# Expert scratch laid into the down weights' place, result stores issued by ScalarE, and routed transposes regrouped, in a Flamingo block with a mixture of experts

## Chip, cores and metric

The kernel runs on one core of a Trainium2 chip. The metric is the device time of one execution in microseconds (us). Engines are named as in the profile: PE is TensorE's matmul, PEld its weight load, DVE VectorE, ACT ScalarE, POOL GpSimd, SP SyncE, which only issues DMAs. A letter q behind an engine means its sequencer.

## The reference

All data is float32. `x` is 8 batches x 512 tokens x 256; `ctx` is 8 x 1024 x 256.

```
x = x + tanh(g0) * attention(layernorm(x), ctx)     # 16 heads of 64, layer norms, rope on the keys
    attn = softmax(clip(q @ k.T * 64**-0.5, -11, 11)); out = (attn @ v) @ Wo + bo
xf = layernorm(x)                                   # 4096 rows of 256
    scores = sigmoid(xf @ router_w.T)               # 64 experts in 8 groups
    the 4 best groups by the sum of their 2 best biased scores, then the 8 best experts in them
    tw = chosen scores / their sum * 2.5
routed = sum over chosen e of tw[e] * (relu(xf @ up_w[e])**2 @ down_w[e])    # 256 -> 128 -> 256
shared = relu(xf @ shared_up)**2 @ shared_down                               # 256 -> 512 -> 256
x = x + tanh(g1) * (routed + shared)
```

## The kernel before

One launch has four stages, each a block of its own in which every engine has its own program; all engines meet between two blocks.

**Setup** (to about 60 us) splits the attention's weights in two parts and turns the rope tables.

**Attention** (60 to 1906 us) goes through 8 batches `b`, in each through 8 pairs of heads `p`, and in each pair through 8 steps `c`. I write (p, c) for a step. A pair is projected while the pair before it attends. In a step PE makes the scores of one tile of 128 context rows (L903), ACT the exponential (L1047), POOL clamps it (L1139), DVE adds it to a sum (L1287), and PE multiplies the clamped tile of two steps earlier with the values (L968). Step 1 also makes the denominators (L976), steps 2 to 4 their reciprocal and the normalised output, steps 5 and 7 the output projection (L1004), which DVE adds to `x1` (L1210). All of it runs in program order on each engine, with semaphores between them.

The routing of the batch before, r = b - 1, is laid between these steps by hand: bias and statistics on DVE at (1, 6) to (2, 1), the reciprocal of the deviation on POOL at (2, 2) (L301, L304), the normalised rows `rows_now` on DVE at (2, 3) and (2, 6) (L312), their transposes on PE at (2, 4) and (3, 4) into the bank `ps_y` (L320), their copies on ACT, the router's product at (4, 4), ranks at (6, 4), and the choice and numbering of slots on DVE. The last of it, `finish_slots`, runs on DVE in pair 0 of the batch after (steps `FINISH`); it gives the row index of each token's 8 copies. Then POOL scatters the normalised rows of that batch into `rows_in_blocks` in DRAM, 32 indirect DMAs of 128 rows (L1119), at 32 steps of pairs 1 to 7, from b = 2 on. Before the first it waits, at the head of (1, 0), for the indices (`slotted`) and the rows (`rows_kept`). For the last batches `finish_slots` runs in the two closing half-pairs.

**Finish of the routing** (1906 to 2051 us): the last batch is routed on DVE (with PE and ACT for the products), POOL scatters the last two batches (64 indirect DMAs, L1387), and for all 8 groups of 512 rows g the shared expert runs: transposes (`turn`), the up product (L1426), relu and square on ACT (L1467, L1471), the down product (L1439), the sum on DVE (L1511). DVE also builds the table of which expert owns which block, and SP loads the up weights of all experts. PE's order is `turn(0)`, the router's transposes, `logits`, then `shared(0)`, `rank`, `shared(1)` to `shared(7)`. The scratch of this stage lies where the next stage puts `down_all`, all experts' down weights (64 x 128 x 256), so `down_all` can only be loaded once the stage is over. The weights of experts 0 to 3 alone are loaded before, into `router.rows`.

**Experts** (2051 to 2510 us): 320 blocks `i` of 128 rows. Blocks 0 to 63 are each expert's first, the rest belong to the expert named by the table. PE transposes the rows (L1770), multiplies by up two blocks later (L1739) and by down four blocks later (L1763). DVE takes relu (L1815) and square (L1819) and copies odd results out of PSUM (L1795), ACT copies the transposed rows (L1722), a table-chosen block's up weights (`now_up`, L1717) and even results (L1703). SP loads rows (L1661, 2 blocks each), loads `down_all` in 16 chunks of 4 experts at blocks 0, 2, ..., 30 (L1681), and stores results 4 blocks at a time (L1668), at block i those of i - 12. For blocks 0 to 47 DVE also puts gates in order (L1803 to L1808). POOL gathers each token's 8 results by 256 indirect DMAs (L1844) into a ring of 8, and DVE adds each to `x1` (L1788), starting at block 112: one per block, and the last 48 after the last block. A gather waits until the sum of 8 gathers before has freed its place.

Of the kernel before, what the change touches and what calls it, by code (L numbers as in the profile page):

```python
# [136 lines left out]
CHUNK = 4  # L137
LAG = 16
# [6 lines left out]
class Routed:  # L145

    def __init__(self, nc, ctx):
# [10 lines left out]
        self.first_loaded = ctx.enter_context(nc.semaphore("first_down_loaded"))  # L158
# [23 lines left out]
class Router:  # L182
# [36 lines left out]
    def scratch(self, nc, ctx, which, x_f, x_nat):  # L219
        def sb(name, shape, dt=F32):  # L220
            return ctx.enter_context(nc.sbuf_tensor(which + name, shape, dt))

        self.x_f, self.x_nat = x_f, x_nat
        self.stats = sb("r_stat", [P, GT, 6])
        self.moments = sb("r_moments", [P, GT, 2])
        self.rstd = sb("r_rstd", [P, 2, GT])
        self.prob = sb("r_prob", [P, GT, E_R])
# [20 lines left out]
        self.settle = sb("r_settle", [P, 1])  # L248
# [458 lines left out]
def attention(nc, pers, rope, ins, wqk_dram, wv_dram, xs_dram, slots_dram, gates_dram, router):  # L707


    with ExitStack() as ctx:  # L710
# [26 lines left out]
        router.scratch(nc, ctx, "a_", affine[:], rows_now[:])  # L737
# [139 lines left out]
        def _(pe):  # L877
# [11 lines left out]
            def step(g, m, c, project, attend, b=None, p=None):  # L889
# [98 lines left out]
                if routed(b) and c == 5 and p in (2, 3):  # L988
                    pe.wait_ge(router.copied, (b - 1) * 2 + p - 1)
# [20 lines left out]
        def _(act):  # L1010
# [16 lines left out]
            def step(g, m, c, project, attend, b=None, p=None):  # L1027
                jj = m % 2
                tail = exists(g - 2)
                if routed(b) and c == 5 and p in (2, 3):  # L1030
                    router.copy(act, b - 1, p - 2, y_flat)
# [52 lines left out]
        def _(pool):  # L1084
# [28 lines left out]
            places = [(p, c) for p in range(1, 7) for c in (0, 1, 4, 5, 7)] + [(7, 0), (7, 1)]  # L1113
            places.sort()
# [7 lines left out]
            def step(g, m, c, project, attend, b=None, p=None):  # L1122

                tail = exists(g - 2)
                if (p, c) == (1, 0) and not isinstance(b, int):
                    pool.wait_ge(router.slotted, b - 1)
                    pool.wait_ge(router.rows_kept, b - 1)
# [16 lines left out]
                if p is not None and not isinstance(b, int) and (p, c) in places:  # L1144
                    scatter(b, places.index((p, c)))
# [11 lines left out]
        def _(dve):  # L1157
# [55 lines left out]
            def route(b, p, c, g):  # L1213
# [16 lines left out]
                if (p, c) == (2, 3):  # L1230
                    router.normalise(dve, 0)
# [27 lines left out]
            def step(g, m, c, project, attend, b=None, p=None):  # L1259
# [53 lines left out]
def finish_routing(nc, pers, ins, kept, router, up, xs_dram, table_dram, slots_dram, gates_dram):  # L1313

    with ExitStack() as ctx:
        def sb(name, shape, dt=F32):
            return ctx.enter_context(nc.sbuf_tensor(name, shape, dt))
# [7 lines left out]
        x_last = sb("x_last", [P, GT, D])  # L1325
        x_f = sb("x_f", [P, 2, C2, TG])
        router.scratch(nc, ctx, "l_", x_f[:, 1], x_last[:])
        x_nat = sb("f_x_nat", [P, RING, GT, D])
        sup = sb("sup", [P, C2, E_S * P])
        sdn = sb("sdn", [P, E_S, D])  # L1330
        h_g = sb("h_g", [P, E_S, TG])
        h_r = sb("h_r", [P, 2, TG])
        total = sb("total", [P, T_T])
        cells = sb("cells", [P, 2, TOP_K, E_R])
        whole = sb("whole", [P, E_R], mybir.dt.int32)
        expert_no = sb("expert_no", [P, E_R])
        block_no = sb("block_no", [P, PACK])
        table_f = sb("table_f", [P, 2, PACK])
        table_t = sb("table_t", [P, 1], mybir.dt.int32)
# [12 lines left out]
        router.gathered()  # L1352

# [52 lines left out]
        def _(pe):  # L1406
# [10 lines left out]
            def shared(g):  # L1417
# [11 lines left out]
                if g + 1 < N_G:  # L1429
                    turn(g + 1)  # L1430
# [22 lines left out]
        def _(act):  # L1453
# [23 lines left out]
            for g in range(N_G):  # L1477
                shared(g)
                if g + 1 < N_G:
                    copies(g + 1)  # L1480
# [416 lines left out]
```

## Time and profile before

| | us |
|---|---|
| median of 3 runs | 2513.14 (2508.35 to 2518.33) |
| the profiled execution's own time | 2512.1 |
| its span in the profile | 2510.3 |
| PE busy | 2284.6 (91%) |
| DVE busy | 2041.2 (81%) |
| POOL busy | 1728.3 (69%) |
| ACT busy | 1522.5 (61%) |
| mean granted TensorE clock | 0.966 |

A busy share is a mean over the four stages; the windows in the section on rows give them apart. The 1.8 us between own time and span lie outside the span.

### The profile page before, as it was taken

What the parts mean: (1) busy time and instruction counts of PE and PEld (TensorE: products, weight loads), DVE (VectorE), ACT (ScalarE), POOL (GpSimd) and SP (SyncE); (2) the same over time, 40 slices, a digit from 0 to 9 for tenths busy, and PEclk for the clock granted to TensorE, in tenths of its full rate; (3) what the DMA queues carried; (4) which work ended last, traced back from release to release, by engine and by line L of the source; (5) the groups of instructions that cost most, each with busy time, mean ns of one, the idle gap of its engine ahead of it and who ended that gap; (6) DMA issues with size and microseconds to landing.
All of it is one profiled execution on the core that took longest, in us unless ns stands there. A gap on an engine that the chain in (4) does not pass through costs nothing. (4 is left out here: it accounts for less than half of the span.)

```text
span 2510.3 us, 40337 instructions
## 1 busy us (share of the span) xinstructions
PE 2284.6 (91%) x11366; PEld 1277.1 (51%) x11366; DVE 2041.2 (81%) x3571; ACT 1522.5 (61%) x2556; POOL 1728.3 (69%) x1515
## 2 busy tenths in 40 slices
PE   3999999999999999999999999999996989998990
PEld 2444445444444444454444444444544668987770
DVE  4778787988988898889889888988886759798884
ACT  4667666756666666667566756666662334766660
POOL 2777585588868876976788688868774600177776
PEclk9999999999999999999999999999997999999995
DMA  9533443111111112111112111111106438799994
GB/s 341 195 123 122 151 145 122 39 61 58 62 48 59 47 57 81 46 59 50 59 45 74 50 60 43 60 57 66 62 26 197 146 104 277 253 333 320 329 319 132
DMA packets 163582, 306.26 MB, mean 122 GB/s; under 512 B 19779, under 2 KB 99587, under 8 KB 160643
## 3 DMA queue, kind: packets, MB, share of 16 engines
q1 hardware_dynamic: 135234, 235.93, 27.5%
q0 software_dynamic: 24576, 67.14, 8.2%
q8 instruction: 105, 1.72, 0.3%
q14 instruction: 147, 1.20, 0.2%
q10 hardware_dynamic: 3520, 0.27, 0.1%
HBM read 173.51 MB, written 129.76 MB: 121 GB/s over the span
## 5 line engine op out<-in xcount | busy, mean ns | idle before, releaser
L1139 POOL TENSOR_SCALAR e<-e 128x1024 f32<-128x1024 f32 x512 | 706.9, 1381 | 320.7 <-ACT e L1047 267.5
L1047 ACT ACTIVATE e<-scores 128x1024 f32<-128x1024 f32 x512 | 524.7, 1025 | 424.3 <-PE scores L903 377.1
L1287 DVE TENSOR_TENSOR e_sum<-e_sum,e 128x1024 f32<-128x1024 f32 x384 | 589.7, 1536 | 100.7 <-POOL e L1139 100.4
L968 PE MATMUL ps_o<-e,v 128*64 128x512 f32 x2048 | 558.2, 624 | 7.8 <-POOL e L1139 7.7
L903 PE MATMUL scores<-q_t,k_t 64*128 64x512 f32 x3072 | 503.5, 433 | 15.1 <-DVE k_t L1277 11.8
L903 PEld LDWEIGHTS scores<-q_t,k_t 64*128 64x128 f32 x3072 | 253.4, 188 | 374.6 <-issue 282.7
L1844 POOL DMA_INDIRECT more<-results_in_blocks,index x256 | 246.0, 961 | 258.4 <-DMA results_in_blocks<-more 176.4
L1065 ACT ACTIVATE k_sw<-ps_k 32x512 f32<-32x512 f32 x512 | 301.3, 589 | 54.3 <-PE ps_k L944 49.2
L1119 POOL DMA_INDIRECT rows_in_blocks<-room,a_r_index_now x192 | 255.5, 1331 | 49.0 <-issue 49.0
L1131 POOL TENSOR_TENSOR k_c<-k_c,k_sw 128x512 f32<-128x512 f32 x128 | 192.6, 1505 | 46.7 <-DVE k_sw L1272 43.9
L944 PE MATMUL ps_k<-ctx_t,wqk 128*128 128x512 f32 x768 | 215.6, 417 | 0.9 <-DVE ctx_t L1163 0.3
L929 PE MATMUL ps_v<-wv,ctx_t 128*128 128x512 f32 x768 | 212.7, 412 | 2.4 <-ACT v L1058 2.4
L968 PEld LDWEIGHTS ps_o<-e,v 128*64 128x64 f32 x2048 | 102.1, 136 | 190.1 <-issue 156.3
L1763 PE MATMUL ps_out<-down_all,room 128*128 (+1 forms) x632 | 192.0, 386 | 0.7 <-DVE room L1819 0.3
L929 PEld LDWEIGHTS ps_v<-wv,ctx_t 128*128 128x128 f32 x768 | 135.0, 189 | 72.0 <-issue 45.5
L944 PEld LDWEIGHTS ps_k<-ctx_t,wqk 128*128 128x128 f32 x768 | 137.7, 193 | 65.8 <-issue 39.1
L1004 PE MATMUL ps_y<-wo,o_n 128*128 128x256 f32 x512 | 148.6, 414 | 13.2 <-DVE x L1210 9.6
L1739 PE MATMUL ps_hid<-x_nat,room 128*128 128x128 f32 x1024 | 157.3, 276 | 0.6 <-DVE room L1815 0.6
L1788 DVE SCALAR_TENSOR_TENSOR x<-more,gate,x 128x256 f32<-128x256 f32 x256 | 123.0, 480 | 42.5 <-DMA more<-results_in_blocks,index 41.5
L1722 ACT ACTIVATE x_nat<-ps_x 128x256 f32<-128x256 f32 x320 | 121.0, 379 | 59.4 <-PE ps_x L1770 56.0
L1277 DVE TENSOR_TENSOR k_t<-k_c,k_t 128x512 fp32r<-128x512 f32 x128 | 122.6, 958 | 41.2 <-ACT k_t L1073 41.0
L1004 PEld LDWEIGHTS ps_y<-wo,o_n 128*128 128x128 f32 x512 | 89.7, 195 | 130.4 <-issue 112.2
(288 smaller groups left out, 3510.5 us busy)
## 6 DMA issues: line engine op xcount, KB each, us to landing
rows_in_blocks<-room SPq DMA_DIRECT2D x16, 2560.0 KB, 10.5
x_nat<-rows_in_blocks SPq DMA_DIRECT2D x160, 256.0 KB, 5.3
results_in_blocks<-more SPq DMA_DIRECT2D x80, 512.0 KB
wqk<-wqk_pairs SPq DMA_DIRECT2D x65, 512.0 KB, 3.5
wv<-wv_quads SPq DMA_DIRECT2D x17, 1024.0 KB, 4.8
x_nat<-in_ctx SPq DMA_DIRECT2D x9, 1024.0 KB, 8.2
wo<-in_L_xattn_Wo SPq DMA_DIRECT2D x66, 128.0 KB, 3.4
down_all<-in_L_ffn_down_w SPq DMA_DIRECT2D x16, 512.0 KB, 7.7
```

What stands on the lines that cost most here:

```text
L903: mm = pe.matmul(scores[:, c % 2, hh * N:(hh + 1) * N], k_t[rows, att, kp, c * P:(c + 1) * P], q_t[rows, att, qp, :], start=(part == 0), s ...
L929: mm = pe.matmul(ps_v[:], ctx_t[:, a, cc, tile * P:(tile + 1) * P], wv[:, bb, cc], start=(k == 0), stop=(k == 5))
L944: mm = pe.matmul(ps_k[:], wqk[:, jj, bb, cc, 1], ctx_t[:, a, cc, half * N:(half + 1) * N], start=(k == 0), stop=(k == 5))
L968: mm = pe.matmul(ps_o[hh * DH:(hh + 1) * DH, :], v[:, tile, buf, hh * DH:(hh + 1) * DH], e[:, tile % 4, hh * N:(hh + 1) * N], start=(tile ...
L1004: mm = pe.matmul(ps_y[:, i, :], o_n[:, t * P:(t + 1) * P], wo[:, jj], start=True, stop=True)
L1047: act.activation(e[:, c % 4], scores[:, c % 2], ACT.Exp, scale=SCALE).then_inc(s_exp, 1)
L1065: st = act.activation(k_sw[to], ps_k[of], ACT.Copy)
L1119: pool.indirect_dma_start(xs_dram, bass.IndirectOffsetOnAxis(ap=router.index_now[:, t, k:k + 1], axis=0), router.rows[:, t], None).then_in ...
L1131: pool.tensor_tensor(k_c[:], k_c[:], k_sw[:], ALU.add).then_inc(s_turned, 1)
L1139: pool.tensor_scalar(e[:, c % 4], e[:, c % 4], EXP_HI, EXP_LO, ALU.min, ALU.max).then_inc(s_clip, 1)
L1287: dve.tensor_tensor(total, e[:, 0] if c == 2 else total, e[:, tile % 4], ALU.add).then_inc(s_sum, 1)
L1844: pool.indirect_dma_start(land[:, k], None, y_dram[0:blocks_of(b, k) * P, :], bass.IndirectOffsetOnAxis(ap=at, axis=0)).then_inc(y_in[k], 16)
```

## The change

1. **Scratch.** `down_all` is allocated ahead of the finish of the routing, and that stage's scratch is cut out of it, in the order in which it comes free. SP can so load chunk 0 after the scatters, chunks 1 to 3 after `last_kept` (ahead of the first rows), chunks 4 to 6 after the last group's transposes (`x_turned`), and chunks 7 to 15 in the experts' stage at blocks 0, 2, ..., 16. The extra load of experts 0 to 3 is gone.
2. **Stores.** ACT issues the stores of results, at block i those of i - 8.
3. **Relu** of blocks 0 to 63 goes from DVE to ACT, behind the copy of block i + 2.
4. **Routed rows** are normalised at (2, 4) and (2, 6) and both transposed in pair 3, at (3, 3) and (3, 4), with the wait for the first copy at (3, 4).
5. **Indices.** POOL waits for them at the first scatter, now (1, 1); the scatter of (1, 0) goes to (7, 5). The last part of `finish_slots` for the last batch but one goes from step 7 to step 2 of the closing half-pair.
6. **Order in the finish.** PE makes the up product of group 0 ahead of the router's transposes, and ACT its relu and square ahead of the router's copies.

```diff
-                if routed(b) and c == 4 and p in (2, 3, 4, 6):
+                if routed(b) and ((p, c) == (3, 3) or c == 4 and p in (3, 4, 6)):
                     pe.wait_ge(s_rec, g + 1)
-                    if p in (2, 3):
-                        router.turn(pe, b - 1, p - 2, y_flat)
+                    if p == 3:
+                        if c == 4:
+                            pe.wait_ge(router.copied, (b - 1) * 2 + 1)
+                        router.turn(pe, b - 1, c - 3, y_flat)
...
-            places = [(p, c) for p in range(1, 7) for c in (0, 1, 4, 5, 7)] + [(7, 0), (7, 1)]
+            places = [(p, c) for p in range(1, 7) for c in (0, 1, 4, 5, 7)][1:] + [(7, 0), (7, 1), (7, 5)]
...
-                if (p, c) == (1, 0) and not isinstance(b, int):
-                    pool.wait_ge(router.slotted, b - 1)
-                    pool.wait_ge(router.rows_kept, b - 1)
...
+                    if (p, c) == places[0]:
+                        pool.wait_ge(router.slotted, b - 1)
+                        pool.wait_ge(router.rows_kept, b - 1)
+                        pool.sem_inc(s_seen, 1)
                     scatter(b, places.index((p, c)))
...
-                if (p, c) == (2, 3):
+                if (p, c) == (2, 4):
                     router.normalise(dve, 0)
...
-                if attend and not project and c in FINISH:
+                if attend and not project and c in FINISH[:-1]:
                     finish_slots(B - 2, FINISH.index(c))
+                if not attend and not project and c == 2:
+                    finish_slots(B - 2, len(FINISH) - 1)
...
+        def load_down(sp, chunks):
+            for k in chunks:
+                sp.dma_start(down[:, k * CHUNK:(k + 1) * CHUNK],
+                             ins["down_w"][k * CHUNK:(k + 1) * CHUNK].rearrange("e p n -> p e n")).then_inc(kept.down_loaded[k], 16)
...
-            sp.dma_start(router.rows, ins["down_w"][0:CHUNK].rearrange("e p n -> p e n")).then_inc(kept.first_loaded, 16)
+            load_down(sp, range(0, ROWS_END))
+            sp.wait_ge(last_kept, 1)
+            load_down(sp, range(ROWS_END, ROUTING_END))
...
+            sp.wait_ge(x_turned, N_G * C2)
+            load_down(sp, range(ROUTING_END, RING_END))
...
             turn(0)
+            ups(0)
             router.turn(pe, last, 0, ps_r[:])
             router.turn(pe, last, 1, ps_l[:])
             router.logits(pe, last, ps_r[:])
-            for g in range(N_G):
-                if g == 1:
-                    router.rank(pe, last, ps_l[:])
-                shared(g)
+            downs(0)
+            router.rank(pe, last, ps_l[:])
+            for g in range(1, N_G):
+                ups(g)
+                downs(g)
...
-                e = i // XC * CHUNK
+                e = (i // XC + RING_END) * CHUNK
...
+            def store(i):
+                for parity in range(2):
+                    act.wait_ge(s_y[parity], (i + YC) // 2)
+                act.dma_start(four_blocks(y_dram, i),
+                              y[:, i % YR:i % YR + YC]).then_inc(y_stored[i % YR // YC], 16)
+
             for i in range(BLOCKS):
+                if i % YC == 0 and i >= 2 * YC:
+                    store(i - 2 * YC)
...
+                j = i - 2
+                if 0 <= j < E_R:
+                    act.wait_ge(s_up, j + 1)
+                    if j >= 2:
+                        act.wait_ge(s_g, j - 1)
+                    act.activation(act_r[:, j % 2], ps_h[:, j % 2, 0:P], ACT.Relu).then_inc(s_relu, 1)
...
-                dve.wait_ge(s_up, i + 1)
-                dve.tensor_scalar(act_r[:, i % 2], ps_h[:, i % 2, 0:P], 0.0, None, ALU.max).then_inc(s_relu, 1)
+                if i >= E_R:
+                    dve.wait_ge(s_up, i + 1)
+                    dve.wait_ge(s_g, i - 1)
+                    dve.tensor_scalar(act_r[:, i % 2], ps_h[:, i % 2, 0:P], 0.0, None, ALU.max).then_inc(s_relu, 1)
```

## Rows read from the trace of the kernel before

**Rows 1.** Windows by stage: length, busy (x instructions) per engine, clock, DMA share, GB/s
```profile
60.00:1906.00 1846.00, 1763.77 (x8249) 852.01 (x8248) 1561.16 (x2175) 1201.99 (x1685) 1397.79 (x1149) 0.98 0.22 73
1906.00:2051.00 145.00, 130.78 (x488) 88.52 (x488) 94.88 (x222) 51.16 (x87) 67.75 (x71) 0.93 0.45 147
2051.00:2124.00 73.00, 64.24 (x429) 55.57 (x430) 63.98 (x179) 28.33 (x82) 0.00 (x0) 0.95 0.85 293
...
2191.00:2452.00 261.00, 238.74 (x1650) 205.59 (x1648) 227.09 (x727) 168.62 (x513) 198.46 (x206) 0.99 0.95 321
```

**Rows 2.** Waits of PE in attention, 300 to 1860 us: total, times, longest
```profile
PE ps_y L320 <- DVE rows_now L312: 22.1, 7, 3.4
```

**Rows 3.** Timeline of PE in one batch, at (2, 4) and (4, 1)
```profile
1249.59 1.11 PE L320 MATMUL ps_y<-ident,rows_now 128*128 128x128 f32 x4 [3.12 <-DVE rows_now L312]
...
1290.62 1.08 PE L976 MATMUL ps_y<-e_sum,ones_dh 128*64 128x512 f32 x4 [1.21 <-DVE e_sum L1287]
```

**Rows 4.** Timeline of POOL in the same batch, clamps of (2, 3) and (2, 4)
```profile
1248.35 2.68 POOL L1139 TENSOR_SCALAR e<-e 128x1024 f32<-128x1024 f32 x2
```

**Rows 5.** Waits of POOL, 1242.9 to 1285.1 us, all there are
```profile
POOL rows_in_blocks L1119 <- issue: 1.7, 7, 0.3
POOL e L1139 <- ACT e L1047: 0.4, 2, 0.3
```

**Rows 6.** Timeline of POOL at (1, 0) of the same batch
```profile
1203.87 1.04 POOL L1139 TENSOR_SCALAR e<-e 128x1024 f32<-128x1024 f32 x1 [4.36 <-DVE index L543]
```

**Rows 7.** The page's group of the scatters in attention: busy, mean ns | idle before
```profile
L1119 POOL DMA_INDIRECT rows_in_blocks<-room,a_r_index_now x192 | 255.5, 1331 | 49.0 <-issue 49.0
```

**Rows 8.** Waits of POOL, 1160 to 1172 us, the end of a batch
```profile
POOL e L1139 <- ACT e L1047: 1.6, 1, 1.6
```

**Rows 9.** Timelines of DVE and PE at attention's end
```profile
1890.72 0.21 DVE L525 TENSOR_TENSOR room<-a_r_at_next,a_r_moved 128x64 f32<-128x64 f32 x1
...
1894.42 1.98 PE L976 MATMUL ps_y<-e_sum,ones_dh 128*64 128x512 f32 x4 [3.30 <-DVE e_sum L1287]
```

**Rows 10.** Timelines of PE and DVE at the start of the finish, and one load's landing
```profile
1922.03 9.70 PE L1426 MATMUL ps_h<-x_f,sup 128*128 128x512 f32 x16
...
1942.13 7.09 PE L1426 MATMUL ps_h<-x_f,sup 128*128 128x512 f32 x16
...
1922.69 0.29 DVE L351 TENSOR_SCALAR l_r_prob<-l_r_prob 128x256 f32<-128x256 f32 x1 [4.79 <-ACT l_r_prob L346]
...
1931.03 0.29 DVE L436 TENSOR_SCALAR l_r_taken<-l_r_gate 128x256 f32<-128x256 f32 x1
...
sdn<-in_L_ffn_shared_down_w SPq DMA_DIRECT2D x1, 512.0 KB, 4.8
```

**Rows 11.** Waits of PE, 2051 to 2191 us
```profile
PE ps_x L1770 <- DMA x_nat<-rows_in_blocks: 7.2, 4, 4.0
```

**Rows 12.** Windows of L1770 alone, two transposes a block
```profile
2062.10:2186.10 124.00, 40.71 (x208) 29.65 (x209) 0.98 0.81 273
2124.00:2186.10 62.10, 21.40 (x112) 15.94 (x113) 1.00 0.77 253
```

**Rows 13.** Timeline of DVE, the relu of two blocks that lie two blocks apart
```profile
2101.84 0.28 DVE L1815 TENSOR_SCALAR room<-ps_hid 128x128 f32<-128x128 f32 x1
...
2104.41 0.28 DVE L1815 TENSOR_SCALAR room<-ps_hid 128x128 f32<-128x128 f32 x1
```

**Rows 14.** Timeline of POOL, the first gather that waits for a sum
```profile
2191.05 0.94 POOL L1844 DMA_INDIRECT more<-results_in_blocks,index  x1 [7.64 <-DVE x L1788]
```

**Rows 15.** SP's issues of stores and of row loads: ns min/median/max
```profile
L1668 SPq DMA_DIRECT2D results_in_blocks<-more x80: 319/320/975, 2060.7 to 2451.7; - x80
...
L1661 SPq DMA_DIRECT2D x_nat<-rows_in_blocks x156: 319/730/2366, 2053.2 to 2438.5; - x156
```

**Rows 16.** Timelines of ACT and DVE around one block of the long loop
```profile
2300.20 0.42 ACT L1717 ACTIVATE room<-up_all 128x256 f32 x1 [0.52 <-issue]
...
2301.75 0.29 DVE L1815 TENSOR_SCALAR room<-ps_hid 128x128 f32<-128x128 f32 x1
```

More of the change, by code:

```diff
@@ L137 @@
 CHUNK = 4
+ROWS_END, ROUTING_END, RING_END = 1, 4, 7
 LAG = 16
@@ L217, in of_tile, with small @@
         return whole[t // LATER][:, t % LATER]
[L219 to L223, printed above, removed]
+    def small(self, sb):
         self.stats = sb("r_stat", [P, GT, 6])
@@ L736, in attention @@
         rows_now = sb("rows_now", [P, GT, D])
-        router.scratch(nc, ctx, "a_", affine[:], rows_now[:])
+        router.small(sb)
+        router.scratch(sb, affine[:], rows_now[:])
         minus_gate = sb("minus_gate", [P, 1])
@@ L987, in step @@
                         router.rank(pe, b - 1, y_flat)
-                if routed(b) and c == 5 and p in (2, 3):
-                    pe.wait_ge(router.copied, (b - 1) * 2 + p - 1)
+                if routed(b) and c == 5 and p == 3:
+                    pe.wait_ge(router.copied, (b - 1) * 2 + 2)
                 if routed(b) and c == 5 and p == 4:
@@ L1029, in step @@
                 tail = exists(g - 2)
-                if routed(b) and c == 5 and p in (2, 3):
-                    router.copy(act, b - 1, p - 2, y_flat)
+                if routed(b) and p == 3 and c in (4, 5):
+                    router.copy(act, b - 1, c - 4, y_flat)
                 if routed(b) and c == 5 and p == 4:
@@ L1473, in _ @@
             copies(0)
-            router.copy(act, last, 0, ps_r[:])
-            router.copy(act, last, 1, ps_l[:])
-            router.tanh(act, last, ps_r[:])
             for g in range(N_G):
                 shared(g)
+                if g == 0:
+                    router.copy(act, last, 0, ps_r[:])
+                    router.copy(act, last, 1, ps_l[:])
+                    router.tanh(act, last, ps_r[:])
                 if g + 1 < N_G:
@@ L1606, in _, with experts @@
             shared(7)
-def experts(nc, pers, ins, out, kept, router, up, xs_dram, y_dram):
+def experts(nc, pers, ins, out, kept, router, up, down, xs_dram, y_dram):
     with ExitStack() as ctx:
@@ L1632, in experts @@
         ps_y = ctx.enter_context(nc.psum_tensor("ps_out", [P, 4, N], F32))
-        down_loaded = [sem(f"down_loaded_{k}") for k in range(E_R // CHUNK)]
+        down_loaded = kept.down_loaded
         x_loaded = kept.x_loaded
@@ L1687, in _ @@
                     finish(b - 2)
-            for i in range(BLOCKS - 3 * YC, BLOCKS, YC):
-                store(i)
             finish(B - 2)
@@ L1877, in program @@
         up = ctx.enter_context(nc.sbuf_tensor("up_all", [P, E_R, D], F32))
-        finish_routing(nc, pers, ins, kept, router, up, xs_dram, table_dram, slots_dram, gates_dram)
-        experts(nc, pers, ins, out, kept, router, up, xs_dram, y_dram)
+        down = ctx.enter_context(nc.sbuf_tensor("down_all", [P, E_R, D], F32))
+        finish_routing(nc, pers, ins, kept, router, up, down, xs_dram, table_dram, slots_dram, gates_dram)
+        experts(nc, pers, ins, out, kept, router, up, down, xs_dram, y_dram)
 def kernel(**inputs):
```

86 lines of the change are left out of this document (48 added, 38 removed).

## The prediction

> **What bounds the kernel now.** I read the windows by stage first. Attention is 1846 us of 2510, with PE busy for 1763.8 of it, so it is PE's stage, with 82 us idle over 8 batches. The finish is 145 us with PE busy 130.8, its idle time at the start. In the experts' stage PE has 9 us idle in the first 73, and from 2191 us on it has 22 idle in 261, but there it isn't the bound: POOL issues 206 gathers in 261 us, one per 1.27 us [rows 1]. The timeline of POOL says since when: at 2191.05 us it last waited, for DVE's first sum [rows 14]. From there 248 of the 256 gathers follow each other; 248 x 1.27 from 2191 is 2506, the span's end but for the last landing and sum. So the end is the moment of the first sum, at block 112, plus 248 gathers. What the change saves ahead of block 112 comes through to the end; what it saves behind it is worth nothing, unless it delays the gathers.
>
> Then I asked for PE's waits in attention, and the largest is the one that part 4 is about: 22.1 us in 7 places for `rows_now` [rows 2]. The question is whether PE gets them back, and the timelines of PE and POOL of one batch answer it.
>
> **Part 4, transposes in pair 3.** PE is idle from 1246.47 us (1249.59 less 3.12) until `rows_now` is there, then makes the transposes (1.11) and the scores of step 5 [rows 3]. Without the wait it makes the scores at once, and then needs POOL's clamp of step 3. POOL starts that at 1248.35 and has it at about 1249.7 (half of 2.68) [rows 4]. So PE resumes 0.1 us later than now, but with the transposes (1.1) and scores (some 1.6 at the low clock after the gap) behind it: 2.7 us won, of which the transposes' 0.6 are paid again in pair 3. That is 2.1 us a batch, and 14.7 us in the seven batches that have routing. That is the upper bound, and I don't take it. From 1242.9 to 1285.1 us POOL never waits: 0.4 us for ACT, and 1.7 in the fixed gaps around its indirect DMAs [rows 5]. POOL is behind with 5 scatters a pair, the norms' reciprocals and the clamps, and at 1290.62 us PE waits 1.21 us for a sum of DVE that hangs on POOL's work of (3, 6) [rows 3]. An earlier PE doesn't make POOL earlier. Only the 0.4 us that POOL waited can be won, and some order between DVE and POOL: 0.5 us a batch. PE's lead turns into waits for clamps in pair 3. The exception is b = 1, where nothing is scattered yet and POOL has time: 2.1 us. Sum 6 x 0.5 + 2.1 = 5.1 us. The new wait for the first copy at (3, 4) is covered by the scores, key product and values product of that step, over 3 us against one copy; if ACT were late by more, PE would pay it.
>
> The Trainium skill (SBUF — State Buffer, "SBUF: two separate sides") says that DVE and GpSimd lock one pair of ports against each other, and the later one waits out the whole instruction. By that rule both saturated engines share one time here, so PE's lead would buy nothing at all, 2.1 us instead of 5.1. The trace leans that way: a clamp that takes 1.04 us elsewhere takes 1.34 in this stretch [rows 4, 6].
>
> **Part 5, the wait for indices.** POOL stands 4.36 us at (1, 0) for the index [rows 6], with the clamp of that step queued behind. PE's waits show nothing for it: its largest in attention is the one above. After the change the wait comes behind two clamps, when the index is there. Worth 0. The scatter moved to (7, 5) costs POOL 1.33 us and 0.26 of gap [rows 7], six times; POOL there still waits 1.6 us for ACT ahead of the clamp of step 5 [rows 8], and behind it PE stands at DVE's key split, so the scatter is covered. Without that cover it would be 6 x 1.6 = 9.6 us slower, the lower bound of this part. The last `advance` at the end stands between 1890.72 us and the sum before the product at 1894.42, on which PE waits 3.30 us [rows 9]: some 1.7 us of small DVE operations leave the path and fall into DVE's idle time behind the reciprocal. 1.7 us won, once.
>
> **Part 6, order in the finish.** Shared up weights land about 4.8 us after the stage's start [rows 10], at 1914 us. The up product of group 0, 9.70 us with the low clock of the start, then ends at 1923.7, where it now ends at 1931.7. The router's transposes, ACT's last square (ahead of the router's copies), the copies, the router's product and the tanh are five short steps in a row, which I put at 1 us each: DVE gets the tanh at about 1928.8 instead of 1922.69. The choice takes DVE 8.6 us, to the mask of L436, and brings it to 1937.4; PE spends that time on the down product, as large as an up product at full clock (7.1), and waits about 1 us. The ranks are 14 small products, which I put at 2.1 us, and the next up product starts at about 1939.6 instead of 1942.13 [rows 10]. 2.5 us won; between 0 (if DVE's scaling of gates, now behind a later mask, holds group 1) and 4. From there the stage is PE's and simply shifts.
>
> **Parts 1 to 3, experts.** From block 8 to 112 there are 208 transposes, 104 blocks, in 124 us. At the pace of the later half (56.5 blocks in 62.1 us, 1.10) they would take 114.3 [rows 12]: 9.7 us lost. Of PE's waits for rows, 7.2 us in four [rows 11], the longest, 4.0 us ahead of block 8, lies outside these 104 blocks. It stays: SP still issues four chunks ahead of the first row load. The low clock behind it (2.5 us) stays too. The other three (3.2 us) fall into the time of the chunks; seven of 16 chunks leave it, 3.7 MB, over 12 us at 293 GB/s [rows 1], so they go. The last 4 us are DVE's: with gate ordering its relus lie 2.57 us apart for two blocks, 1.29 a block against PE's 1.10 [rows 13]. The relu of 0.28 (0.31 with its gap) less gives 0.98, under PE. So 7.2 us can be won; ACT, busy 28.3 of 73 us [rows 1], has room for relu and stores. I take 7.0; the lower bound is 3 (only one of the two works).
>
> The stores: SP's issue takes 0.32 us [rows 15]. On ACT the wait for DVE's odd result and the issue stand ahead of `now_up` and the copy of block i. The loop closes once in four blocks: DVE's result, issue (0.32), `now_up` to relu 1.55 [rows 16], two blocks of DVE at 1.10 (227.1 us for 206 blocks), its result copy 0.4: about 4.3 us. POOL's pace leaves 4 x 1.27 = 5.1 [rows 1]. Covered by 0.8 us, so 0; the gathers set the time anyway.
>
> The Trainium skill (DMA: Bandwidth & Descriptors, "Issuing engines are not separate DMA queues") has it that another issuing engine saves only the issue time. By it the stores bring nothing; my sum has 0 for them too, and the third rival stands against both.
>
> **Sum.** 5.1 + 1.7 + 2.5 + 7.0 = 16.3 us. The profiled execution took 2512.1 us, 1.0 below the median of the runs; less 16.3 it is 2495.8. Its own range, from the bounds of the middle terms, is 2489 to 2503.
>
> **Rivals.**
> - *PE gets the whole gap back.* POOL's load isn't fixed, since clamps are shorter when DVE isn't at them: 14.7 instead of 5.1 us, 2486 us. For it: PE is busy 96% of the stage. Against it: [rows 5]. 0.15.
> - *The savings don't arrive.* The later mask delays the finish and SP's nine remaining chunks keep the early experts bound by transfers: 3 of 7.0, 0 of 2.5, 2 of 5.1: 2505 us. For it: the four chunks ahead of the first rows are unchanged. 0.18.
> - *ACT's stores hold the loop (slower).* An issue of SP's row loads takes 0.73 in the median and up to 2.37 us [rows 15]; if ACT's take longer than 0.32 + 0.8 = 1.1 us, the loop passes the gathers and sets the pace. At 2.0 us the four blocks take 6.0 instead of 5.1, 0.22 a block, over 206 blocks 46 us: 2542 us. Against it: the issues of the same stores on SP, median 0.32. 0.07.
>
> **How the numbers follow.** Forecast 0.60, rivals 0.15, 0.18, 0.07. Below 0.5%, 12.6 us, a measurement of this kernel can't tell a difference; the limit is 2500.5 us. Faster: 0.9 of the forecast and the first rival, 0.69. Same: the rest of the forecast and most of the second, 0.23. Slower 0.08. The range of 8 in 10 goes from the first rival's time to the second's: 2485 to 2507.
>
> **What would show it.** PE's wait for `rows_now` gone, with waits for clamps (L968 on L1139) grown in pair 3, and a batch's period down by 0.5 and not by 2 us; POOL's first wait at (1, 1) near 0; group 1's up product 2.5 us earlier behind the stage's start; blocks 8 to 112 in about 117 us, with the 4 us wait ahead of block 8 still there; gathers at 1.27 us. Wrong it would be by a gather pace over 1.3 us (ACT's stores), or by a batch's period down by 2 us (POOL not the bound).

## The result, and the profile after

The changed kernel takes 2522.2 us in the median of 9 runs (2517.5 to 2525.7), the kernel before 2512.7 beside it: a ratio of 1.0042, 95% interval 1.0031 to 1.0052. It is 9.5 us slower, where 16 us faster was forecast. The profiled execution's own time is 2521.93 us, its span 2520.2, which is 9.9 over the span before. The windows by stage, which answer to [rows 1]:

```profile
60.00:1911.00 1851.00, 1766.42 (x8250) 850.12 (x8248) 1559.41 (x2175) 1203.63 (x1686) 1386.48 (x1149) 0.98 0.21 73
...
2196.00:2457.00 261.00, 233.95 (x1621) 198.43 (x1620) 226.00 (x710) 155.37 (x504) 197.27 (x203) 1.00 0.95 316
```

The last row is the first finding: 203 gathers in 261 us, where there were 206, and PE is busy for 234.0 us of it, where it was 238.7. The long stretch at the end has become slower, though nothing was to change in it.

I cut both traces at five events: PE's denominators in the last whole pair, PE's first instruction of the finish and of the experts, the first gather that waits for a sum, and the last gather.

| us | before | after | difference | forecast |
|---|---|---|---|---|
| to the last whole pair's denominators | 1869.5 | 1876.1 | +6.6 | -5.1 |
| from there to the finish | 40.9 | 39.2 | -1.8 | -1.7 |
| finish | 140.8 | 138.6 | -2.1 | -2.5 |
| experts to the first waiting gather | 139.9 | 141.9 | +2.1 | -7.0 |
| the gathers (247 intervals) | 312.7 | 317.7 | +5.0 | 0 |

Two rows are as forecast, and three have the wrong sign or a cost where none was seen. I found two causes. The first row by itself doesn't show one: in eleven more profiles of kernels without part 4 the last whole pair's denominators come anywhere from 1869.1 to 1878.9 us. What singles part 4 out is the time with one line of it undone (a4) and the sum of pairs 2 and 3, both below.

**Attention.** PE's waits from 300 to 1860 us, where [rows 2] came from:

```profile
PE ps_o L969 <- POOL e L1138: 22.9, 18, 2.6
PE ps_y L977 <- DVE e_sum L1290: 20.1, 15, 2.6
```

The 22.1 us for `rows_now` are gone, but PE's waits for the clamp grew from 6.0 to 22.9 us, and those for the sum from 11.9 to 20.1. The timeline of PE in the batch of [rows 3] shows where:

```profile
1251.86 1.98 PE L969 MATMUL ps_o<-e,v 128*64 128x512 f32 x4 [2.08 <-POOL e L1138]
...
1268.10 1.38 PE L977 MATMUL ps_y<-e_sum,ones_dh 128*64 128x512 f32 x4 [2.29 <-DVE e_sum L1290]
```

And DVE in the same stretch, before and after:

```profile
1247.60 1.93 DVE L312 TENSOR_SCALAR rows_now<-x,a_r_moments,a_r_rstd 128x256 f32 x2 [0.91 <-POOL a_r_rstd L304]
```

```profile
1251.93 2.07 DVE L1290 TENSOR_TENSOR e_sum<-e_sum,e 128x1024 f32<-128x1024 f32 x1 [2.22 <-POOL e L1138]
1253.92 1.16 DVE L312 TENSOR_SCALAR rows_now<-x,r_moments,r_rstd 128x256 f32 x2
```

The normalisation used to fill DVE's wait for the clamp. Moved one step on, it leaves 2.22 us of DVE idle and stands in the busy stretch behind it. Then the windows of pair 2 (to its denominators) and pair 3 of one batch, first before, then after; the eighth column is the granted clock:

```profile
1003.37:1033.66 30.29, 26.13 (x116) 11.58 (x114) 25.04 (x39) 16.59 (x24) 26.57 (x27) 0.89 0.13 45
1033.66:1058.59 24.93, 23.74 (x116) 10.55 (x114) 22.14 (x26) 17.67 (x27) 22.92 (x19) 1.00 0.17 58
```

```profile
1003.54:1033.85 30.31, 23.46 (x112) 10.11 (x108) 25.21 (x39) 17.32 (x24) 26.78 (x27) 0.99 0.14 48
1033.85:1061.11 27.26, 27.18 (x118) 12.22 (x118) 21.42 (x26) 16.54 (x25) 20.92 (x19) 0.89 0.13 41
```

Pair 2 takes 30.3 us in both: DVE and POOL set it. Pair 3 takes 27.26 instead of 24.93, with PE busy 27.18 of it at a mean clock of 0.89. Over the six batches with scatters pair 2 went from 182.0 to 181.8 us in all and pair 3 from 149.6 to 156.1, together from 331.6 to 337.9. In the twelve profiles of kernels without part 4 this sum is 330.5 to 333.7, in the four with part 4 as changed (the changed kernel, a1, a3, f2) 335.5 to 338.6: these don't overlap.

**Experts.** Blocks 8 to 112, transposes alone, beside [rows 12]:

```profile
2064.60:2191.10 126.50, 40.90 (x208) 28.00 (x209) 0.99 0.73 243
```

It took 124.0 us before and was to take 117. What PE waits for from 2190 to 2460 us was nearly all DMA (18.9 us, 21 times); after:

```profile
PE ps_x L1809 <- ACT x_nat L1757: 26.7, 51, 0.6
```

Every fourth block PE waits half a microsecond for ACT's copy. The timelines of one such place, of DVE, ACT and PE, show the loop behind it:

```profile
2299.83 0.42 DVE L1834 COPY more<-ps_out 128x256 f32<-128x256 f32 x1
...
2300.33 0.33 ACTq L1735 DMA_DIRECT2D results_in_blocks<-more  x1
2301.21 0.42 ACT L1752 ACTIVATE room<-up_all 128x256 f32 x1 [2.02 <-PE ps_hid L1782]
2301.53 0.36 ACT L1757 ACTIVATE x_nat<-ps_x 128x256 f32<-128x256 f32 x1
...
2302.05 0.41 PE L1809 MATMUL ps_x<-ident,x_nat 128*128 128x128 f32 x2 [0.55 <-ACT x_nat L1757]
...
2302.94 0.29 DVE L1856 TENSOR_SCALAR room<-ps_hid 128x128 f32<-128x128 f32 x1 [0.50 <-PE ps_hid L1782]
...
2304.97 0.41 DVE L1834 COPY more<-ps_out 128x256 f32<-128x256 f32 x1
```

From one result copy of DVE to the next but one it is 5.14 us: 0.50 to the issue, 0.88 from there to `now_up` (the issue's 0.33 and 0.55 in which ACT also loads the table's register), 1.73 to relu, 2.03 to the next copy. Four gathers at 1.266 us are 5.06. So the loop, not POOL, sets the pace: 317.7 / 247 = 1.286 us a gather.

### The profile page after: what moved, and what is told of

The parts are those of the page before. It is cut to its first block and busy times, and to the rows that moved or that the text cites. A ratio compares the mean times of both kernels' runs of the same rounds, so it can differ in the third digit from the quotient of the medians.

```text
span 2520.2 us, 40661 instructions
## 1 busy us (share of the span) xinstructions
PE 2285.4 (91%) x11366; PEld 1266.0 (50%) x11366; DVE 2025.4 (80%) x3507; ACT 1521.7 (60%) x2620; POOL 1719.5 (68%) x1515
## 3 DMA queue, kind: packets, MB, share of 16 engines
q14 instruction: 150, 1.22, 0.2%
## 5 line engine op out<-in xcount | busy, mean ns | idle before, releaser
L1068 ACT ACTIVATE k_sw<-ps_k 32x512 f32<-32x512 f32 x512 | 301.3, 589 | 58.1 <-PE ps_k L945 53.1
L1121 POOL DMA_INDIRECT rows_in_blocks<-room,r_index_now x192 | 252.7, 1316 | 50.6 <-issue 47.9
L1130 POOL TENSOR_TENSOR k_c<-k_c,k_sw 128x512 f32<-128x512 f32 x128 | 186.0, 1453 | 41.9 <-DVE k_sw L1275 39.0
L1752 ACT ACTIVATE room<-up_all 128x256 f32 x256 | 106.8, 417 | 124.2 <-PE ps_hid L1782 108.7
L945 PEld LDWEIGHTS ps_k<-ctx_t,wqk 128*128 128x128 f32 x768 | 138.4, 193 | 66.3 <-issue 39.2
L1809 PE MATMUL ps_x<-ident,x_nat 128*128 128x128 f32 x640 | 124.8, 277 | 38.4 <-ACT x_nat L1757 33.3
```

What stands on the lines that cost most here:

```text
L945: mm = pe.matmul(ps_k[:], wqk[:, jj, bb, cc, 1], ctx_t[:, a, cc, half * N:(half + 1) * N], start=(k == 0), stop=(k == 5))
L1068: st = act.activation(k_sw[to], ps_k[of], ACT.Copy)
L1121: pool.indirect_dma_start(xs_dram, bass.IndirectOffsetOnAxis(ap=router.index_now[:, t, k:k + 1], axis=0), router.rows[:, t], None).then_in ...
```

## Experiments

Each was timed beside the kernel before on its chip; the ratio is to that. Where two kernels are compared by stages, these are cut from their profiles as above. On two of the chips the kernel before took 2658.7 and 2651.3 us; there I read ratios, the attention and the blocks ahead of 64 alone (the last section says why).

### One part alone, or undone

The kernel before with parts 4 and 5 alone (a1) and with part 2 alone (a2), by the lines of the diff above; the changed kernel with the stores taken from ACT's program and put back into SP's (a3):

```diff
-                if i % YC == 0 and i >= 2 * YC:
-                    store(i - 2 * YC)
...
+                if i % YC == 0 and i >= 3 * YC:
+                    store(i - 3 * YC)
```

And the changed kernel with one line back (a4):

```diff
-                if (p, c) == (2, 4):
+                if (p, c) == (2, 3):
                     router.normalise(dve, 0)
```

> The kernel before with parts 4 and 5 alone (the attention). Theory: the normalisation moved from (2, 3) to (2, 4) leaves DVE idle ahead of the sum of step 3 and comes back as a wait of PE for the sum at the denominators; it carries the whole loss of the attention, which ends 4.8 us later in the trace after (1915.2 instead of 1910.4), and nothing behind it moves: 2512.7 + 4.8 = 2517.5 us. Rival, the attention's delay in the trace comes from the new place of the scratch (parts 1 to 3 and 6): 2512.7 us or, by my prediction's terms, 2506.

2514.96 us, ratio 1.0014 (1.0004 to 1.0024). Pair 3 of the six batches took 153.7 us against 149.6. Slower with no change of scratch: the loss is in parts 4 and 5, and by pair 3 in part 4. 3.5 us is less than the 4.8 forecast; in this profile two of six third pairs escaped the low clock.

> The kernel before with part 2 alone (ACT issues the stores). Theory: the store waits for DVE's odd result ahead of the copies that PE needs; four blocks take 4.75 instead of 4.4 us ahead of block 112 (48 blocks from 64 on, +4.3 us) and gathers come every 1.286 instead of 1.266 us behind it (248, +5.0 us): 2512.7 + 9.3 = 2522 us. Rival, as the prediction had it: the loop has 0.8 us to spare and an issue costs only its 0.33 us: 2512.7 us.

2520.85 us, ratio 1.0030 (1.0019 to 1.0041). Blocks 64 to 112 take 57.3 us as in the changed kernel (52.8 before), and 201 gathers fit in 261 us:

```profile
2193.70:2454.70 261.00, 232.50 (x1611) 197.48 (x1610) 223.80 (x705) 154.50 (x501) 195.92 (x201) 1.00 0.94 314
```

Experts to the last gather take 461.9 us against 452.6, the 9.3 us of the theory. The store's place alone makes the slower loop.

> The changed kernel with part 2 undone (SP stores again, those of i - 12 at block i), all else as changed. Theory: 9.3 us come back, 2522.2 - 9.3 = 2512.9 us, with gathers at 1.27 us and blocks 64 to 112 at 1.10. Rival, the loss of the experts' stage comes from relu on ACT or the down loads on SP: 2522 us.

2507.6 us, ratio 0.9978 (0.9967 to 0.9989): 14.6 us under the changed kernel, more than the 9.3 expected. Blocks 8 to 112 take 116.6 us instead of 126.5, and the gathers 312.7. The stores also covered up what relu and loads win in blocks 8 to 64, which here came out for the first time.

> The changed kernel with only the normalisation of the first half of the rows back at (2, 3); transposes still in pair 3. Theory: DVE makes it while it waits for the clamp, the wait of PE for the sum at (3, 1) (2.2 to 2.6 us) goes, a batch takes 232 us or up to 0.5 less, as predicted for part 4: 6 to 9 us back, 2513 to 2516 us. Rival, PE's lead over POOL or the two transposes close together in pair 3 cause the loss: it stays at 2522 us.

2515.98 us, ratio 1.0014 (1.0004 to 1.0024) in place of 1.0042: 6 us back. But only part of the mechanism was as I had it. Pair 2 takes 29.7 us now, in all six batches, 0.6 less than before, since DVE's wait is filled again. PE still waits up to 2.0 us for the sum behind it, and pair 3 still takes 26.0:

```profile
1002.72:1032.42 29.70, 23.51 (x113) 10.12 (x109) 25.52 (x39) 17.23 (x24) 26.15 (x26) 1.00 0.14 49
1032.42:1058.43 26.01, 25.93 (x118) 11.45 (x118) 21.63 (x26) 16.50 (x25) 22.49 (x19) 0.93 0.13 47
```

So a second cause may be left: PE's idle time now lies at the end of pair 2.

### Is it where PE idles?

The kernel a4, with a wait of PE added and nothing moved (d1), and later both with the stores on SP (e2, and without the wait e1):

```diff
+                if routed(b) and (p, c) == (2, 4):
+                    pe.wait_ge(router.normed, (b - 1) * 2 + 1)
```

> The kernel with the normalisation back at (2, 3) (2516 us), and PE made to wait at (2, 4) for the first normalised rows, as it did before, though it transposes them only in pair 3. In the traces the pair that the wait lies in takes 30.3 us with it and 29.7 without, as POOL and DVE let it; without it PE stands 2.0 us at that pair's end, its granted clock is 0.93 or 0.89 in pair 3 in place of 1.00, and pair 3, which PE bounds, takes 26.0 or 27.3 us in place of 24.95. Theory (the place of PE's idle time decides, through the clock): the added wait puts the low clock back into pair 2 and gives pair 3 back its 25 us; the attention ends 2 to 4 us earlier, 2512 to 2514 us. Rival (the loss is in moving transposes and scatters, not in the clock): 2516 to 2518 us.

2665.54 us beside 2658.69, ratio 1.0031 (1.0020 to 1.0042). By the time the forecast of 2 to 4 us failed, as a4's ratio was 1.0014; but the two were timed on different chips, this one on a chip where the end of the kernel is slower, so it decides nothing. The attention's windows do. The low clock is back in pair 2 and away from pair 3:

```profile
1004.38:1034.69 30.31, 26.09 (x112) 11.42 (x110) 25.39 (x39) 16.03 (x23) 26.57 (x26) 0.89 0.12 45
1034.69:1059.61 24.92, 24.33 (x120) 10.96 (x119) 22.13 (x26) 18.02 (x28) 22.91 (x19) 1.00 0.17 57
```

All six third pairs take 24.9 to 25.0 us; pairs 2 and 3 together 330.3 us, against 332.9 without the wait (a4) and 331.6 in the kernel before. Then the pair with the stores on SP, side by side:

> The changed kernel with the stores on SP and the normalisation at (2, 3); the transposes stay in pair 3. The two repairs lie in different stages and should add: 2507.6 - 6.5 = 2501 us, pair 2 of a batch about 29.7 us, pair 3 about 26.0. If the stages weren't independent it would be 2507 us.

> The same with PE made to wait at (2, 4) for the first normalised rows. In its trace with the stores on ACT every pair 3 took 25.0 us and pair 2 30.1. Theory (PE's idle time at the end of pair 2 lowers the clock in pair 3, which PE bounds): 2 to 3 us faster than without the wait, 2498 to 2499 us, no slower than the kernel with the attention as before. Rival (a wait more is only a wait): equal or slower, 2501 to 2504 us.

Beside a kernel before of 2651.3 us, 2648.5 without the wait (ratio 0.9986, 0.9974 to 0.9998) and 2645.9 with it (0.9978, 0.9968 to 0.9988). The times alone don't decide it, as the intervals overlap; the direction and size, 2.6 us, are the theory's. The traces do: four of six third pairs at 26.0 us without the wait, none with it, and pairs 2 and 3 together 331.9 us without it and 330.4 with it. So 1.5 us of the 2.6 is seen where the theory has it. Both ratios are above the forecasts, which come to 0.996 (2501 of 2511 us) and 0.995; on this chip the stages behind the attention take longer.

Over all profiles of this study, in the orders that leave PE idle at the end of pair 2 (the changed kernel and five more) 30 of 36 third pairs took 25.8 us or more; in the two with the added wait none of 12; in the kernel before and eleven with its order of routed rows 15 of 72. The granted clock tells the last 15 apart. Its mean was 0.89 to 0.94 in those 30 third pairs, and 1.00 in all others: the 6 that escaped, the 12, and all 72 of the old order. The 15 took 25.9 us at full clock, each behind a pair 2 of 30.8 or 30.9 us, and I don't know their cause. Nor does PE's wait bring the low clock each time. The 6 that escaped had waits of 2.5 us (three) and 1.6 us (three) ahead of them; the shortest wait with the low clock behind it was 1.7 us.

### The loop of the stores

SP stores, and ACT only waits where it would store (s1, against the kernel before); ACT stores one block later (s2, against a2); ACT stores at the same block, behind the register's load (s3, against a2; `keep`, the copy of an even result, goes behind the load with it):

```diff
+                if i % YC == 0 and i >= 2 * YC:
+                    for parity in range(2):
+                        act.wait_ge(s_y[parity], (i - YC) // 2)
```

```diff
-                if i % YC == 0 and i >= 2 * YC:
-                    store(i - 2 * YC)
+                if i % YC == 1 and i >= 2 * YC:
+                    store(i - 1 - 2 * YC)
```

```diff
-                if i % YC == 0 and i >= 2 * YC:
-                    store(i - 2 * YC)
-                if i >= 5 and i % 2:
-                    keep(i - 5)
...
                         packed = act.snap(four, min_val=0, max_val=E_R ** PACK - 1)
+                if i % YC == 0 and i >= 2 * YC:
+                    store(i - 2 * YC)
+                if i >= 5 and i % 2:
+                    keep(i - 5)
```

> The kernel before, stores still issued by SP, and ACT only waits at the place where it would issue them. In the trace after, four blocks close a loop of 5.14 us: DVE's result copy, 0.50 from its start to the issue, 0.88 from the issue to now_up, 1.73 from there to relu, 2.03 from relu to the next result copy. Theory A (wait and issue only together exceed the 5.06 us that four gathers take): without the issue the loop is 4.8 us, under 5.06, and the time stays at 2511 us, gathers at 1.27 us. Theory B (the wait alone does it): 2519 to 2521 us, gathers at 1.286 us.

> The kernel before with the stores on ACT, but at blocks 1 modulo 4 (those of i - 9) instead of 0 modulo 4. Theory (a loop closes over the wait for DVE's latest odd result): with a block more between the result and the store, 1.1 us or more of it leaves the loop, and the time is that of before, 2511 us, gathers at 1.27 us. Rival (issuing 80 stores costs ACT's program its time wherever it stands): 2519 to 2521 us.

> The kernel before with the stores on ACT at blocks 0 modulo 4, but behind the load of the table's register, which otherwise follows the store and is most of the 0.5 us between the issue's end and now_up. Theory: the load then runs while ACT waits for DVE's result, the loop is 4.6 instead of 5.14 us, and the time is 2511 to 2513 us. Rival (the gap behind the issue belongs to the issue itself): 2519 to 2521 us.

Beside 2512.5 us: 2513.0 (ratio 0.9997, 0.9984 to 1.0009), 2512.1 (0.9993, 0.9980 to 1.0005) and 2513.8 (0.9996, 0.9981 to 1.0011). By the terms above each took one part of the loop away, 0.33, 1.1 or some 0.5 us. Blocks 64 to 112 took 53.1, 52.8 and 52.9 us. From the experts' start to the last gather it was 454.6, 452.3 and 455.0 us, where a2 took 461.9 and the kernel before 452.6: 7 to 9.6 of the 9.3 us were gone. So theory A holds: the wait alone costs 2 us at most, and wait and issue together 2.4 or nothing once the loop is shorter. In s3 a gather still took 315.4 / 247 = 1.277 us, a loop just at the edge. s2's profile is of the slowest of its 12 runs, 2520.8 us, the very time that the rival forecast; but its attention, which is that of before, ends 8.9 us later, and its experts' stage is as short as before. In the changed kernel itself both repairs together (f2), the store of `i - 1 - 2 * YC` at blocks 1 modulo 4 behind the register's load, `keep` again with it:

> The changed kernel with the one edit that the store stands at blocks 1 modulo 4 and behind the load of the table's register. Theory (it is the place of the store, not the engine): as with the stores on SP, blocks 64 to 112 in 52.8 us in place of 57.3, blocks 8 to 112 in 116.5 in place of 126.5, ratio to before 0.998 (with stores on SP it was 0.9978). Rival (with relu too, ACT's program is full in the first 64 blocks): blocks 16 to 48 at 40 us and a ratio of 1.000 or more.

2506.93 us, ratio 0.9984 (0.9975 to 0.9992), blocks 8 to 112 in 117.8 us and 207 gathers in 261 us: 15 us under the change, with the stores still on ACT. Blocks 16 to 48 take 36.9 us, 1.0 more than with the stores on SP, and blocks 8 to 64 65.0 us, 1.2 more.

The same repair in the kernel c1 (below), which has the stores on SP (d4):

> The same best kernel with the stores on ACT after all, but at blocks 1 modulo 4 and behind the load of the table's register. Theory: 1.1 us and 0.5 us leave the loop, so ACT's stores cost nothing and, as the prediction had it, bring nothing: 2500.7 us within 1.5. Rival (SP, free of stores, loads rows earlier and the stores are worth something after all): 2497 us or less. Rival (with relu on ACT too, its program is too full): 2503 us or more.

2657.1 us beside 2658.7, ratio 0.9991 (0.9979 to 1.0003). Behind block 64 this chip sets another pace; ahead of it blocks 16 to 48 take 35.7 us, as with the stores on SP, and blocks 8 to 64 64.9 us, where d2, with the stores on SP on the same chip, takes 63.7. No gain from ACT's stores shows anywhere; a cost of 1 us in the first blocks may be left.

### Relu and the down loads

The kernel c1 (below) with part 3 undone on two chips (d3, e3), and the kernel before with part 3 alone (f1), each by the last two hunks of the diff above:

```diff
-                if i >= E_R:
-                    dve.wait_ge(s_up, i + 1)
-                    dve.wait_ge(s_g, i - 1)
-                    dve.tensor_scalar(act_r[:, i % 2], ps_h[:, i % 2, 0:P], 0.0, None, ALU.max).then_inc(s_relu, 1)
+                dve.wait_ge(s_up, i + 1)
+                dve.tensor_scalar(act_r[:, i % 2], ps_h[:, i % 2, 0:P], 0.0, None, ALU.max).then_inc(s_relu, 1)
```

> The same best kernel with part 3 undone (DVE takes relu of all blocks). It splits the 7.4 us that blocks 8 to 112 won. Theory, by the prediction's terms: relu on ACT is worth 4 us, the earlier down loads 3.2: 2504 to 2505 us. Rival 1 (the loads are all of it): 2500.7 us. Rival 2 (relu on ACT is all of it): 2508 us.

> The kernel with part 4, the scatters' places and part 2 undone (2500.7 us), and part 3 undone too (DVE takes relu of all blocks), on a chip whose kernel before takes about 2512 us. Theory, by the prediction's terms: relu on ACT is worth 4 us and the earlier down loads 3: 2504 to 2505 us. Rival 1 (the loads are all of it): 2501 us. Rival 2 (relu is all of it, as the trace of the same kernel on a slower chip has it, where blocks 16 to 48 take 40.7 us in place of 36.0): 2506 to 2508 us.

> The kernel before with part 3 alone (relu of blocks 0 to 63 on ACT); scratch, down loads, stores and finish as before. With relu back on DVE the blocks 8 to 64 took 71.2 us, with all down loads early, as much as before (71.3), and 63.8 with relu on ACT. Theory (relu is all of it, the early loads nothing): blocks 8 to 64 in 64 us, 7 us or 0.3% under before. Rival (relu is worth it only once the loads are out of the way, that is, chunks and rows on SP bind next): 66.5 us or more for blocks 8 to 64, 0 to 5 us under before.

The first two are one kernel on two chips: ratios 0.9999 (0.9989 to 1.0008) and 0.9986 (0.9973 to 0.9999). In both, blocks 8 to 64 take 71.2 us, as before (71.3), though all down loads are early; with relu on ACT too they take 63.8. Relu on ACT alone gives 67.2, in the third kernel. So relu is worth 4.1 us, the loads 3.4 on top of it, and nothing without it. (The two with relu on DVE ran on the chips of 2658.7 and 2651.3 us, from which there is no profile of the kernel before; but with relu on ACT these blocks took 64.0 us there (e4), against 63.8.) In f1 the waits for rows stand where they were, 6.8 us in 5, beside 7.2 in 4 of [rows 11]. The theory that relu is all of it fell; the rival (chunks and rows bind next) is right. End to end f1 took 2510.5 us, ratio 0.9998 (0.9989 to 1.0007): in its profile the attention, which is that of before, ended 3.3 us later, and 4 us in one stage is less than I can show by the time.

### What is left together

The changed kernel without part 2, part 4 and the scatters' places of part 5 (c1, again as e4), and c1 with these places (d2):

```diff
-            places = [(p, c) for p in range(1, 7) for c in (0, 1, 4, 5, 7)] + [(7, 0), (7, 1)]
-            places.sort()
+            places = [(p, c) for p in range(1, 7) for c in (0, 1, 4, 5, 7)][1:] + [(7, 0), (7, 1), (7, 5)]
```

> The changed kernel with part 4, the scatters' places of part 5 and part 2 undone; left of the change are the scratch and early down loads, relu on ACT, the finish's order and the earlier end of the slots of the last batch but one. Theory: attention ends 1 to 2 us earlier than before, the finish is 2.1 us shorter, the experts' stage 8.4 us shorter up to the first gather that waits for a sum, gathers come at 1.266 us: 2511.0 - 12 = 2499 us. Rival, the losses of the attention come from the scratch's new place and not from part 4: 2505 us or more.

2500.7 us in 6 runs, ratio 0.9945 (0.9924 to 0.9966), the fastest of all and faster than both kernels. Experts to the first waiting gather take 132.3 us, gathers 312.1, the finish 138.6.

> The kernel with part 4, the scatters' places and part 2 undone, beside the three others on one chip: 2500 to 2501 us, 0.45% to 0.5% under before, and 4 to 7 us under the one with relu on DVE.

2644.7 beside 2651.3 us, ratio 0.9974 (0.9962 to 0.9987): smaller there, and 6.3 us under the one with relu on DVE, in medians. The one with the added wait (e2, 0.9978) is as fast within the noise, as its forecast had it.

> The best kernel so far (2500.7 us: part 4, the scatters' places and part 2 undone) with the scatters of part 5 put back in (first at (1, 1) with the wait for indices, the last at (7, 5)). Theory, as in the prediction: worth 0, 2500.7 us within 1.5. Rival (part of the attention's loss comes from the scatters): 1 us or more slower, up to the 9.6 us of the prediction's bound.

2655.3 beside 2658.7 us, ratio 0.9984 (0.9971 to 0.9997). Against e4's 0.9974 on another chip the difference is 2.7 us, with intervals of 3 us and more on each. The profiles settle more: the finish starts at 1912.5 us here, and at 1913.2 and 1912.9 in the two kernels with the old places on this chip (d3, d4). The bound of 9.6 us is excluded.

## Why the prediction was wrong

**What bounds the kernel** stood up as far as it went: the end is the first sum plus the gathers. The step behind it, "what it saves behind it is worth nothing, unless it delays the gathers", named the case that came.

**The stores: the step that failed.** "about 4.3 us", and "Covered by 0.8 us, so 0", was the step; the loop took 5.14 us. The terms as printed (0.32, 1.55, 2.2, 0.4) add up to 4.47, so 0.17 was lost in the adding. 0.55 is the time behind the issue, in which ACT loads the register: [rows 16] had its 0.52 ahead of `now_up`, and I began the term behind it. The rest is 0.18 more from `now_up` to relu, 0.10 more ahead of the issue, less 0.17 for DVE's two blocks. And the cover was only named for the part of the stage that has gathers. Ahead of block 112 there are none; there the bound is PE's 4.4 us for four blocks, and without DVE's sums the loop took 57.3 / 12 = 4.77. So the stores cost 9.9 us ahead of block 112 (126.5 against 116.6) and 5.0 behind it. The third rival was this mechanism, but its condition, an issue of over 1.1 us, was wrong: 0.33 was enough. The page "DMA: Bandwidth & Descriptors" of the Trainium skill ("Issuing engines are not separate DMA queues"), by which another issuing engine saves only the issue time, agrees with the runs on the gain: f2 and d4 show none. What the stores cost here lies elsewhere, in the copies behind an issue that waits.

**Part 4: wrong sign.** The first half was right to 0.1 us: PE's product with the clamped tile came 2.8 us earlier in the pair (14.05 instead of 16.83 us behind the denominators), where 2.7 was worked out, with a wait of 2.08 us for the clamp ahead of it. That POOL and DVE would take it back was right too. What failed is "PE's lead turns into waits for clamps in pair 3" and the 0.5 us a batch. The lead was gone by the end of pair 2, as a wait for DVE's sum, and that place is worse than the old one: behind a wait of 3.12 us in pair 2 the low clock fell on a pair that DVE and POOL bound; behind 2.2 to 2.6 us at its end it fell, in five of six batches, on pair 3, which PE bounds. I had counted idle time and not where the slow clock behind it lands. And I had moved the normalisation without a cost, although DVE waits there. With it at (2, 3), pair 2 took 29.7 us, 178.1 in six batches against 179.4 to 182.3 in the twelve profiles with the old order, which is about the 0.5 us a batch of the forecast.

The Trainium skill's rule of the shared port ("SBUF — State Buffer", "SBUF: two separate sides") had been used to put the gain of these batches at nothing. The rule itself agrees with the trace: at 1264.96 us of the changed kernel a clamp starts 0.11 us behind a sum of DVE of 1.22 us, and takes 2.01 us where it takes 1.04 alone. It holds, by the page, against DVE's operations in its two-port modes and those with two inputs in SBUF, such as this sum. What doesn't follow is that the pair can't get shorter: DVE still stood waiting for POOL, 2.22 us in the changed kernel, and with that wait filled pair 2 took 0.5 to 0.6 us less.

**Attention's end and the finish: right.** 1.8 us against 1.7, and 2.1 against 2.5 in these two profiles. DVE gets the tanh 18.2 us behind the stage's start, where 18.4 was worked out, and group 1's up product starts 29.4 behind it instead of 31.7:

```profile
1933.40 0.29 DVE L351 TENSOR_SCALAR down_all<-down_all 128x256 f32<-128x256 f32 x1 [10.68 <-ACT down_all L346]
...
1944.60 5.80 PE L1460 MATMUL ps_h<-down_all 128*128 128x512 f32 x13
```

Other profiles make the second gain smaller: on chips of about 2512 us the old order of the finish took 139.2 to 140.8 us, the new one 138.6 to 138.9. The end of the attention took 40.0 to 40.9 us in the old order and 36.9 to 39.3 in the new one.

**Parts 1 to 3: right, under the stores' cost.** Without these, blocks 8 to 112 take 116.6 us where 117 was forecast, and 7.4 us are won for 7.0. The split is right as well, 4.1 and 3.4 for 4.0 and 3.2, with the condition that the loads bring nothing alone.

**Part 5: right.** POOL's 4.36 us at (1, 0) are gone; its first scatter at (1, 1) follows 0.27 us behind the clamp. The scatters' new places show no cost (d2).

Of 16.3 us forecast, the 11.2 outside part 4 came. The changed kernel shows 9.5 us slower because 15 us for the stores and some 6 for part 4 stand against them. Part 4's share is the less certain: 6 us by a4 and by pairs 2 and 3, while parts 4 and 5 together cost 3.5 in a1, with the gain at the attention's end in it.

## What to carry to other kernels

When a DMA issue moves to another engine's program, price the whole loop that its waits close, from the result it waits for to the next one, with everything behind it in that program, and compare it in each stretch with what bounds that stretch; a bound that covers it at one place is absent at another. When a wait of the matmul engine is removed, ask where its idle time goes: here a stretch that other engines bound carried the low clock for nothing, and a stretch that the matmuls bound took 1 to 2.3 us more. And ask of a moved instruction whether it filled a wait where it stood.

## What the runs showed of the hardware

- The granted clock made an added wait worth having: with it pairs 2 and 3 took 330.3 us instead of 332.9 for six batches (d1, a4), and 330.4 instead of 331.9 (e2, e1). In the orders with PE idle ahead of it a third pair had three lengths, 24.9, 26.0 and 27.3 us, with mean clocks of 1.00, 0.93 and 0.89.
- Two chips ran the same kernel before in 2658.7 and 2651.3 us. Attention and blocks 8 to 64 took as long there. The stretch of the gathers did not: 261 us of the fastest kernel (e4) held 156 gathers at 243 GB/s there, where [rows 1] has 206 at 321, as its windows show, and an edit to the block loop is worth less. The finish took 187 to 191 us instead of 139. What sets the pace there is open. The DMA engines aren't it alone, as they were busy 0.75 of the 261 us instead of 0.95, and moved as much per busy time (243 / 0.75 = 324, 321 / 0.95 = 338 GB/s). In the same 261 us DVE and ACT wait 110 us in all for events to which the profile of e4 gives no instruction; the profile of the same kernel on the faster chip (c1) has no such wait.

```profile
2239.00:2500.00 261.00, 207.08 (x1251) 168.67 (x1250) 172.72 (x544) 126.44 (x393) 148.05 (x156) 0.95 0.75 243
```
